# Mixture-of-experts layers on one core: narrow experts in two halves of 224 columns instead of 280 and 168

## What is computed

```python
# layer 0: rows of x gathered per expert, at most cap = 560 each
xg = x_pad[dispatch]                                            # [8, 560, 256]
h = _gelu(jnp.einsum('ecd,edf->ecf', xg, w1) + b1[:, None, :])  # [8, 560, 1024]
y = jnp.einsum('ecf,efd->ecd', h, w2) + b2[:, None, :]
out = segment_sum(y * g[..., None])                             # added to x by token
# layer 1
h = _silu(jnp.einsum('th,ehf->etf', x, w1)) * jnp.einsum('th,ehf->etf', x, w3)
out = jnp.einsum('etf,efh,te->th', h, w2, w)
```

## Time and profile before

| | us |
|---|---|
| median of 3 runs | 1078.6 (1077.78 to 1078.62) |
| profiled execution | 1077.01, its span 1075.2 |
| TensorE matmul busy | 949.4 (88%) |
| VectorE busy | 686.7 (64%) |
| ScalarE busy | 544.9 (51%) |
| GpSimd busy | 475.3 (44%) |

### The profile page before, as it was taken

The page is one execution under the profiler, slowest core; times in us unless marked ns, Lnnn a source line. Parts: engine busy times, 40 slices in busy tenths (PEclk is TensorE's granted clock), DMA queues, the critical chain, the costliest instruction groups (busy, mean ns, idle before and its releaser), DMA issues.

```text
span 1075.2 us, 23113 instructions
## 1 busy us (share of the span) xinstructions
PE 949.4 (88%) x8011; PEld 872.3 (81%) x8011; DVE 686.7 (64%) x1937; ACT 544.9 (51%) x1212; POOL 475.3 (44%) x462
## 2 busy tenths in 40 slices
PE   4889999999999668999999847973999999999998
PEld 4778888778887458999999825763999999999997
DVE  6456676676666666666666635875667788777242
ACT  3678888878888544555455422421334333433110
POOL 2022225234223247666666621475356455545423
PEclk9799999999999869999899968975999999999999
DMA  6878888887774166767676676545254335433101
GB/s 188 164 206 192 204 196 216 231 206 171 194 184 110 52 193 174 185 161 164 168 173 170 153 176 172 189 144 167 99 143 103 101 110 154 114 102 80 21 3 23
DMA packets 109669, 160.09 MB, mean 149 GB/s; under 512 B 11360, under 2 KB 98624, under 8 KB 107616
## 3 DMA queue, kind: packets, MB, share of 16 engines
q1 hardware_dynamic: 95600, 140.03, 49.7%
q0 software_dynamic: 13936, 18.33, 8.6%
HBM read 103.32 MB, written 56.96 MB: 149 GB/s over the span
## 4 chain that ended last, share of the span: by engine, by line
PE 47%; DVE 5%; issue 4%; DMA 3%; POOL 3%; ACT 2%; POOLq 0%; SPq 0%; ACTq 0%; DVEq 0%
PE ps L302 37%; PE ps L597 2%; PE ps L580 2%; DVE HTH L1317 2%; DMA x_scratch<-YY,XG 2%; POOL x_scratch L1588 2%; PE ps L651 1%; PE ps L492 1%; DVE WL L924 1%; PE ps L316 1%; POOL HTL L1576 1%; DMA XG<-xg_scratch 1%; ACT GT L820 1%; POOL xg_scratch L1524 1%; PE ps L588 1%
## 5 line engine op out<-in xcount | busy, mean ns | idle before, releaser
L302 PE MATMUL ps<-XGH,WH 128*128 128x280 f32 (+1 forms) x768 | 225.2, 293 | 9.4 <-ACT GT L820 7.4
L302 PE MATMUL ps<-XGL,WH 128*128 128x280 f32 (+1 forms) x768 | 224.2, 292 | 0.0
L302 PE MATMUL ps<-XGH,WL 128*128 128x280 f32 (+1 forms) x768 | 224.1, 292 | 0.0
L1576 POOL TENSOR_TENSOR HTL<-GT,HTH 128x280 fp32r<-128x280 f32 x128 | 133.6, 1057 | 168.4 <-DVE HTH L1317 168.4
L1189 DVE CUSTOM_DVE_ANT_0 NS<-ps,negm 112x375 f32<-112x375 f32 x256 | 137.9, 545 | 91.3 <-PE ps L408 90.3
L302 PE MATMUL ps<-WH,HTH 128*112 128x256 f32 x568 | 162.3, 286 | 1.9 <-DVE YY L1331 1.5
L302 PEld LDWEIGHTS ps<-XGH,WH 128*128 128x128 f32 x768 | 149.1, 194 | 14.2 <-ACT GT L820 10.7
L302 PE MATMUL ps<-WL,HTH 128*112 128x256 f32 x568 | 159.7, 281 | 0.0
L302 PE MATMUL ps<-WH,HTL 128*112 128x256 f32 x568 | 159.6, 281 | 0.0
L748 ACT ACTIVATE PP<-NS,MN 112x375 f32<-112x375 f32 x256 | 156.8, 613 | 3.5 <-DVE MN L1189 3.0
L302 PEld LDWEIGHTS ps<-XGH,WL 128*128 128x128 f32 x768 | 149.3, 194 | 0.0
(11 more groups left out here) (208 smaller groups left out, 1887.4 us busy)
## 6 DMA issues: line engine op xcount, KB each, us to landing
WG<-in_v SPq DMA_DIRECT2D x48, 512.0 KB, 4.1
KST<-k_scratch SPq DMA_DIRECT2D x48, 376.0 KB, 5.4
WG<-in_w SPq DMA_DIRECT2D x32, 512.0 KB, 5.0
k_scratch<-KHL SPq DMA_DIRECT2D x64, 188.0 KB
CT<-in_ctx_t SPq DMA_DIRECT2D x32, 375.0 KB, 7.1
xg_scratch<-zero SPq DMA_DIRECT2D x8, 1289.8 KB, 10.3
xg_scratch<-zero SPq DMA_DIRECT2D x16, 586.2 KB, 9.3
XG<-xg_scratch SPq DMA_DIRECT2D x14, 586.2 KB, 4.5
```

Source lines behind the costliest of these rows:

```text
L302: m = e.matmul(out_ap, l, r, start=n == 0, stop=n == len(steps) - 1)
L1576: e.tensor_tensor(HTL[:, f, cols], GT[:, gi % 3, :], HTH[:, f, cols], ALU.subtract).then_inc(hl_pool[layer], 1)
```

## The change

The columns of an expert are laid out as blocks 0, 1, 4, 2, 3. A narrow expert has its tokens in blocks 0 to 3, so its first half is columns 0 to 223 and its second 336 to 559, 224 each. A wide expert has two halves of 280 as before, and both hold part of block 4. The first half now lies inside the branch as well, in both bodies. A wide expert waits for all three pieces of its input before the first half; a narrow one waits for the first piece before the first half and for the second before the second. In PSUM a narrow first half writes columns 0 to 223 of a bank and a narrow second half 56 to 279; ScalarE, VectorE and GpSimd still read 280. Four matmuls ahead of layer 0 write columns 224 to 279 of the four banks once, so that they are defined.

```diff
+        def row_cols(c, n=1):
+            o = (0, S, 3 * S, 4 * S, 2 * S)[c]
+            return slice(o, o + n * S)
...
             def hidden(ex, hf, width):
-                cols = slice(hf * HALF, hf * HALF + width)
+                c0 = hf * (HALF - width)
+                cols = slice(hf * HALF + c0, hf * HALF + c0 + width)
...
-                        three(ps[:, bk, 0:width], pairs, e).then_inc(h_mm[layer], 1)
+                        three(ps[:, bk, c0:c0 + width], pairs, e).then_inc(h_mm[layer], 1)
...
+            if layer == 0:
+                e.wait_ge(min_done, N)
+                e.wait_ge(cp_done, N)
+                for bk in range(4):
+                    e.matmul(ps[:, bk, NARROW // 2:HALF], ident, cst[:, 0:HALF - NARROW // 2], start=True, stop=True)
             for c0 in (0, 2, 4):
                 transposes(0, c0)
             for ex in range(E):
                 if ex == 0:
                     e.wait_ge(r_fl, layer + 1)
-                e.wait_ge(xgl[layer], 3 * ex + 2)
-                hidden(ex, 0, HALF)
-                e.wait_ge(xgl[layer], 3 * (ex + 1))
                 with e.If(e.value_load(fl[0:1, layer, ex:ex + 1], min_val=0, max_val=1)):
+                    e.wait_ge(xgl[layer], 3 * (ex + 1))
+                    hidden(ex, 0, HALF)
                     hidden(ex, 1, HALF)
                 with e.Else():
-                    hidden(ex, 1, NARROW - HALF)
+                    e.wait_ge(xgl[layer], 3 * ex + 1)
+                    hidden(ex, 0, NARROW // 2)
+                    e.wait_ge(xgl[layer], 3 * ex + 2)
+                    hidden(ex, 1, NARROW // 2)
```

More of the change, by code:

```diff
@@ L536, in rows_out @@
                     o = slice((k % 4) * D, (k % 4 + 1) * D)
-                    pairs.append(((HTH[:, k, c * S:(c + 1) * S], HTL[:, k, c * S:(c + 1) * S]), (hi[:, o], lo[:, o])))
+                    pairs.append(((HTH[:, k, row_cols(c)], HTL[:, k, row_cols(c)]), (hi[:, o], lo[:, o])))
                 if full:
@@ L807, in gathered_hi @@
                     e.wait_ge(h_mm[layer], 16 * (1 + layer) * ex)
-                e.activation(XGH[:, :, c0 * S:(c0 + n) * S], ps[:, bk, 0:2 * n * S].rearrange("p (k s) -> p k s", k=2),
+                e.activation(XGH[:, :, row_cols(c0, n)], ps[:, bk, 0:2 * n * S].rearrange("p (k s) -> p k s", k=2),
                              ACT.Copy).then_inc(xgh[layer], 1)
@@ L1299, in gathered_lo @@
                 n = min(2, 5 - c0)
-                o = slice(c0 * S, (c0 + n) * S)
+                o = row_cols(c0, n)
                 bk = 6 + banks.at["g", layer, ex, c0][0]
```

## The result

The change makes the kernel slower: 1095.9 us (median of 4, 1094.5 to 1097.1) against 1078.2 (1074.6 to 1078.6), a ratio of 1.016, 95% interval 1.013 to 1.020. Forecast were 1070.1 and a range that ends at 1075.

What follows compares the result with a forecast made beforehand. Bound: TensorE's hidden matmuls in layer 1, with a floor of about 111 ns each, but not in layer 0's hidden stage. 6.9 + 0.5 - 1.3 - 0.3 + 2.7 = 8.5 us off 1078.6 gives 1070.1, range 1066.5 to 1075.

Steps and rivals of the forecast that it cites:

- Part 1: Narrow experts' hidden matmuls: 224 + 224 columns at 111.4 ns each save 6.9 us in layer 1, 0.5 in layer 0.
- Part 2: Wide experts start only when all three input pieces are split; late third pieces cost 1.3 us over both layers.
- 6.9 - 0.7 - 0.3: Layer 1: 6.9 us gained by the widths, 0.7 lost at expert 0's start and 0.3 at expert 6's.
- Part 3: Register load and branch moved ahead of the first half: hidden by queued work, 0.3 us only at layer 0's first expert.
- rival D: Longer jumped-over bodies need a code fetch: 2.1 us in each of eight layer-1 experts, 16.8 us, 1086.9; chance 0.12.
- Part 4: Layer 0, expert 4: the clock's fall to half, costing 3.6 us, goes or shortens; 2.7 us gained.
- 0.5 - 0.3 - 0.3 + 2.7: Layer 0: expert 3's widths gain 0.5 us, waits cost 0.3, the branch at the first expert 0.3, the clock gains 2.7.
- the term of 0.5: Layer 0, expert 3: the first half's last unit comes 0.8 us earlier for ScalarE, 0.5 us kept.
- rival B: Layer 0: clock stays low as long in expert 4, or also falls in expert 1: 1072.8, up to 1075; chance 0.22.

Runs made afterwards that it cites:

- e1: Changed kernel with the widths written into the program, no register load or branch ahead of the hidden matmuls: 1067.5 us, ratio 0.990.
- e2: Kernel before with the second half's width written into the program in place of its branch: 1077.8 us, ratio 0.9989.
- e4: Kernel before plus a never-entered branch over 192 matmuls and their loads ahead of each expert of layer 1: ratio 1.034.
- e5: Kernel before plus a never-entered branch over 96 matmuls and their loads ahead of each expert of layer 1: ratio 1.001.
- e11: Kernel before plus a never-entered branch over 144 matmuls and their loads ahead of each expert of layer 1: ratio 1.012.
- e3: Changed kernel with each half in a branch of its own, same widths and waits: 1073.6 us, ratio 0.996.
- e7: Changed kernel plus one never-entered branch over 64 matmuls and loads ahead of layer 0, moving later code 128 instructions on: ratio 1.017.
- e8: Changed kernel with the flag inverted, so the narrow body lies first and the wide one behind it: ratio 1.005.
- e9: Changed kernel with each half in a branch of its own and the narrow body first in both: 1068.7 us, ratio 0.989.

## Why the prediction was wrong

**Part 1, the widths: right.** 224 columns cost 21.44 / 192 = 111.7 ns (forecast 111.4), 1.6 us an expert. In e1 the wait of experts 2 and 4 grew from 0.54 to 1.28 us, by the 0.7 us that their first 42 matmuls became shorter, as forecast.

**Part 2, the waits: right.** In e1 expert 6 starts 0.75 us late, and the wait of 0.54 us that followed is gone. Layer 1 went from 324.6 to 318.8 us without these branches, 5.8 less, where the terms 6.9 - 0.7 - 0.3 add up to 5.9.

**Part 3, the branch: this step failed.** It was put at nothing, because the branch between the halves left no gap and because 2.3 us of work are queued at the new place. The first reading is right (e2), and the second fits (e4's 4.1 to 4.9 us out of 6.9), but neither bounds the new jump. The first was of a jump over 96 matmuls, the new one is over 192, and the price rises steeply between the two (e5, e11, e4). The text said that the bodies double and sent that to rival D. In its place the runs show 17.8 us of gaps in layer 1, in which TensorE waits for code, and about 12 us for the clock: 27.7 us together, as the waits of 1.28 us disappear in them.

**Rival D was what happened, at a chance of 0.12 and undersized.** Its price of 2.1 us came from a small data transfer; the jump measured 6.9 to 7.4 us uncovered. It left 1086.9, 9 us under the result, and had no term for the clock, although the 10 us at half clock behind a wait of 1.40 us in the earlier trace rows stood among the rows. The gaps themselves, 17.8 us, are near its 16.8, but by luck: a price of a third of the real one was put without any cover on all eight experts. What it lacked is the clock's 12.

The rule that the prediction gave as speaking for D, that a taken branch whose target is outside a window of two pages of 256 instructions stalls for a fetch (the Trainium skill, Runtime: NRT & Kernel Launch, Instruction fetch mechanics), agrees in kind: a jump over 192 instructions mostly leaves no gap, one over 384 mostly does. It deserved far more than 0.12. An estimate from the page's figures is that a jump over 192 never misses and one over 384 does about every second time; the runs have 1 and 7 of 8 (e5, e4). The measurements decide: jumps over 192 instructions stall at times too, also in e3 (0.67, 1.67 and 1.14 us) and in layer 0 of e7. The "mostly miss" that the prediction read from the rule for 384 is more than the rule gives, though it is what came.

**Part 4, the clock in layer 0: about right, with luck in it.** The wait ahead of the second half of expert 4 grew to 2.12 us, the clock fell at about 511 us and was back at about 514.4, 3.4 us instead of 10. Layer 0 became 2.5 us shorter; forecast, all its terms, were 0.5 - 0.3 - 0.3 + 2.7 = 2.6. It was gained in experts 4 and 5; expert 3 took 12.40 us after 12.39, so that the term of 0.5 gave nothing. And the 2.5 hang on the one profile of the kernel before: in e2, e4, e5 and e11, whose layer 0 has the same widths, it takes 232.8 to 233.2 us instead of 230.4, with a second stretch of 10.2 us at half clock in expert 1. The fall in expert 1 that rival B feared came in e1, e3, e8 and e9, but for 3.4 us only.

So without the failed step the sum stands: e1 measured 1067.5, forecast was 1070.1, with the range from 1066.5.

## What to carry to other kernels

Count the length of a branch's body in instructions as a cost of its own: on TensorE a jump over a body of 192 instructions mostly left no gap here, at times one of 0.7 to 3.3 us, and one over 384 left up to 7 us, less with work queued. "No gap at today's branch" bounds only a jump of today's length, and of today's place in the code. If two cases need different sizes, keep what is common outside, cut one long body into several short ones, and put the frequent case first, so that the jump falls behind its work. A gap of some microseconds on TensorE can cost again by the clock: 2.7 us behind the 3.73 us in expert 1.

## What the runs showed of the hardware

- Price of a jump over 384 instructions with an empty queue: 6.86 us (e4) and 7.35 (e8). It does not follow the number of jumps (e3, e9) but length (e5, e11, e4) and place in the code (e7). TensorE starts again 1.2 to 1.8 us after a packet of code has landed (34 gaps). In e4 the packet itself starts 4.1 us after TensorE ran dry; what sets that, and why less is lost behind the second half, is open.
- Skipped code is fetched too: 69 packets of 16.4 KB on the code queue without the hidden branches (e1, e2), 78 before, 88 after, 91 in e4.
- The profile can name an engine for a gap that is a wait for code: 2.04 us under `XGL`, 1.78 us under `HTL`.
- Behind the wait in expert 4 of layer 0 TensorE was at half clock for 10.2 us with matmuls of 168 columns (before, e2, e4, e5, e11) and for 3.4 us with 224 (after, e1, e3, e8, e9). At half clock both start 213 ns apart, at full clock 111 to 112.
